# Graph network on one core: the second phase of the edge pass sums in PSUM over four node tiles per bank

## The reference, cut to what matters

```python
h = jnp.concatenate([x[row], edge_attr], axis=1)
h = jax.nn.relu(h @ W1a + b1a) @ W1b + b1b
sums = jax.ops.segment_sum(h, col, num_segments=n_nodes)
...
agg = sums / jnp.clip(counts, 1.0)[:, None]
z = jnp.concatenate([x, agg, u[batch]], axis=1)
return jax.nn.relu(z @ W2a + b2a) @ W2b + b2b
```

## Time and profile before

| what | us |
|---|---|
| median of 3 runs | 9276.49 (9272.69 to 9281.15) |
| profiled execution, its own time | 9279.41 |
| its span in the trace | 9277.6 |
| second block and tail, 8981.7 to the end | 295.9 |
| of it, the matmuls of the second block | 8995.5 to 9242.7 |
| TensorE busy in the whole span | 6981.1 (75%) |
| VectorE busy in the whole span | 5643.3 (61%) |
| ScalarE busy in the whole span | 2493.9 (27%) |
| mean granted clock of TensorE | 0.872 |

### The profile page before, as it was taken

How to read it: one execution, slowest core, us unless ns; L and a number is a source line. 1 busy time by engine, 2 the same in 40 slices (tenths; PEclk the granted TensorE clock), 3 DMA queues, 4 the chain that set the end, 5 groups by cost and what they waited for, 6 DMA issues and landing times. The chain is left out here.

```text
span 9277.6 us, 133405 instructions
## 1 busy us (share of the span) xinstructions
PE 6981.1 (75%) x35552; PEld 4550.7 (49%) x35552; DVE 5643.3 (61%) x16834; ACT 2493.9 (27%) x5841; POOL 2675.9 (29%) x2953
## 2 busy tenths in 40 slices
PE   4777777775566669960388779999998777777779
PEld 3555555543122224430277734444445666666668
DVE  6777777775589991039899920000012777777778
ACT  0222222222457750020288700000000333330000
POOL 0777777776461000000000000000001444444430
PEclk9776767776679999985699989999999999999999
DMA  3333333334975547849666658788887766762256
GB/s 99 100 104 105 104 105 104 105 103 140 392 257 165 166 123 276 300 171 426 245 215 215 193 192 282 250 295 272 269 282 229 181 181 179 180 159 63 64 98 197
DMA packets 969801, 1759.60 MB, mean 190 GB/s; under 512 B 102719, under 2 KB 665300, under 8 KB 905490
## 3 DMA queue, kind: packets, MB, share of 16 engines
q1 hardware_dynamic: 683996, 1335.60, 44.5%
q0 software_dynamic: 110720, 276.01, 9.2%
q10 hardware_dynamic: 174394, 139.51, 5.6%
HBM read 1411.91 MB, written 338.80 MB: 189 GB/s over the span
## 5 line engine op out<-in xcount | busy, mean ns | idle before, releaser
L768 POOL DMA_INDIRECT bucketed<-arena,wide x1563 | 1516.6, 970 | 729.9 <-issue 717.1
L1869 PE MATMUL psum<-wide,arena 128*128 x6496 | 1210.1, 329 | 401.2 <-DVE arena L1928 389.4
L1869 PEld LDWEIGHTS psum<-wide,arena 128*128 128x128 f32 x6496 | 988.5, 195 | 621.2 <-issue 494.9
L1738 POOL DMA_DIRECT2D table<-wide x13 | 9.7, 744 | 4325.3 <-DVE wide L1650 4325.3
L1928 DVE TENSOR_SCALAR arena<-wide,tile_first 128x128 f32 x3248 | 869.1, 301 | 471.2 <-PE psum L1869 298.2
L1790 POOL DMA_INDIRECT arena<-table,src_i x832 | 801.1, 963 | 1010.9 <-PE psum L1886 875.1
L1599 PE MATMUL psum<-arena,h 128*128 128x512 f32 (+1 forms) x2548 | 1049.5, 571 | 16.8 <-DMA arena<-adjacency 15.0
L922 PE MATMUL psum<-arena 128*128 128x512 bf16 x2304 | 698.1, 437 | 433.7 <-DVE arena L870 257.7
L665 PE MATMUL psum<-arena 128*113 128x177 bf16 x1568 | 532.4, 340 | 430.8 <-ACT wide L687 388.8
L870 DVE TENSOR_SCALAR arena<-sums 128x512 bf16<-128x512 int16 x2304 | 803.6, 349 | 0.0
L659 PE MATMUL psum<-w_edge,arena 128*128 128x256 f32 x1568 | 786.0, 597 | 0.0
(11 more groups left out here) (398 smaller groups left out, 10879.1 us busy)
## 6 DMA issues: line engine op xcount, KB each, us to landing
arena<-adjacency SPq DMA_DIRECT2D x294, 1024.0 KB
arena<-adjacency SPq DMA_DIRECT2D x98, 1568.0 KB, 7.8
adjacency<-wide SPq DMA_DIRECT2D x588, 256.0 KB
arena<-adjacency SPq DMA_DIRECT2D x196, 640.0 KB, 5.2
arena<-adjacency SPq DMA_DIRECT2D x147, 768.0 KB
arena<-bucketed POOLq DMA_DIRECT2D x208, 528.0 KB, 6.1
arena<-adjacency SPq DMA_DIRECT2D x49, 1792.0 KB, 6.8
arena<-adjacency SPq DMA_DIRECT2D x49, 1344.0 KB, 6.1
```

What stands on the lines that cost most here:

```text
L768: e.indirect_dma_start(bucketed, bass.IndirectOffsetOnAxis(ap=places[k][0:size, c:c + 1], axis=0), rows[k][0:size, c, :], None).then_inc(s ...
L1869: e.matmul(flat[:, ds((chunk & 3) * 512 + 2048, P)], lhsT=hot[:, i % 8, :], rhs=table_in[:, ds(tile * P, P)], start=False, stop=True, skip ...
```

## The change

TensorE now sums in PSUM over all pairs of a tile, and a bank of 512 columns holds the four tiles of a group. ScalarE fills a bank with the group's part of `h` ahead (`begin`), and copies it back to `h` when the last pair of the group is done. It waits for TensorE's count of pairs against a register; those 13 ends of groups (`group_end`) are computed by four new steps in `positions`. TensorE reads each pair's tile number into a register: two bits of it and the bits above give the column and the bank of the sum and the group that must be open. The first block of the edge pass is unchanged. VectorE has only the one-hots left, four pairs (eight chunks, 128 x 1024) in one instruction, in four buffers.

```diff
         last_i = sb("last_i", [1, TILES], i32)[:, :]
+        group_end = sb("group_end", [1, 16], i32)
...
+            ("vector", lambda e, _: e.tensor_copy(pair_end, last), 1),
             ("vector", lambda e, _: e.tensor_scalar(last, last, -1.0, 0.0, op0=ALU.add, op1=ALU.max), 1),
+            ("tensor", lambda e, _: e.matmul(psum[0:1, 1, 128:128 + TILES], lhsT=pair_end, rhs=ident[0:TILES, 0:TILES], start=True, stop=True), 1),
+            ("vector", lambda e, _: e.memset(group_end[:, GROUPS - 1:GROUPS], FAR_PAIRS + NEAR_PAIRS), 1),
+            ("vector", lambda e, _: e.tensor_scalar(group_end[:, 0:GROUPS - 1], psum[0:1, 1, 128 + GROUP - 1:128 + TILES - 1:GROUP], float(NEAR_PAIRS),
+                                                    float(FAR_PAIRS), op0=ALU.min, op1=ALU.add), 1),
...
                     for n in range(NEAR_PAIRS):
                         g = n // 2
+                        if n % DEEP == 0:
+                            _, tile = nc.values_load_multi_w_load_instructions(
+                                tile_i[0:1, n:n + DEEP], engines=(ENG.PE,), min_val=0, max_val=TILES - 1,
...
                         if n % 2 == 0:
                             e.wait_ge(near_got[g % DEEP].sem, near_got[g % DEEP].at + 16 * (g // DEEP) + 16)
-                        e.wait_ge(near_hot_done.sem, near_hot_done.at + n + 1)
-                        if n >= DEEP:
-                            e.wait_ge(near_add.sem, near_add.at + n - DEEP + 1)
+                        if n % QUAD == 0:
+                            e.wait_ge(near_hot_done.sem, near_hot_done.at + n // QUAD + 1)
+                        e.wait_ge(near_open.sem, (tile[n % DEEP] >> 2) + (near_open.at + 1))
                         for c in range(PAIR):
                             at = (n % 2 * PAIR + c) * P
-                            last = e.matmul(psum[:, n % DEEP, 0:P], lhsT=near_in[:, g % DEEP, at:at + P], rhs=near_hot[:, n % DEEP, c, :],
-                                            start=c == 0, stop=c == PAIR - 1)
+                            last = e.matmul(flat[:, ds((tile[n % DEEP] & 15) * P, P)], lhsT=near_in[:, g % DEEP, at:at + P],
+                                            rhs=near_hot[:, n // QUAD % 4, n % QUAD * PAIR + c, :], start=False, stop=True, skip_group_check=True)
                         last.then_inc(near_pe.sem, 1)

                 @block.vector
                 def _(e):
-                    def one_hots(n):
-                        if n >= DEEP:
-                            e.wait_ge(near_pe.sem, near_pe.at + n - DEEP + 1)
-                        e.tensor_tensor(near_hot[:, n % DEEP, :, :], iota[:, 0:P].unsqueeze(1).broadcast_to([P, PAIR, P]),
-                                        dst_f[:, cols(n)].unsqueeze(2).broadcast_to([P, PAIR, P]), ALU.is_equal).then_inc(near_hot_done.sem, 1)
-
-                    def add(n, tile):
-                        e.wait_ge(near_pe.sem, near_pe.at + n + 1)
-                        if n:
-                            e.wait_ge(near_add.sem, near_add.at + n)
-                        to = h[:, ds(tile, 1), :].rearrange("p a n -> p (a n)")
-                        e.tensor_tensor(to, to, psum[:, n % DEEP, 0:D], ALU.add).then_inc(near_add.sem, 1)
...
+                    for n in range(0, NEAR_PAIRS, QUAD):
+                        if n >= 4 * QUAD:
+                            e.wait_ge(near_pe.sem, near_pe.at + n - 3 * QUAD)
+                        e.tensor_tensor(near_hot[:, n // QUAD % 4, :, :], iota[:, 0:P].unsqueeze(1).broadcast_to([P, QUAD * PAIR, P]),
+                                        dst_f[:, cols(n, QUAD)].unsqueeze(2).broadcast_to([P, QUAD * PAIR, P]), ALU.is_equal).then_inc(near_hot_done.sem, 1)
+
+                @block.scalar
+                def _(e):
+                    def begin(g):
+                        a, n = dst_groups[g]
+                        e.copy(psum[:, g % 4, 0:n], part(h, a, n)).then_inc(near_open.sem, 1)
+
+                    for g in range(4):
+                        begin(g)
+                    _, end = nc.values_load_multi_w_load_instructions(
+                        group_end[0:1, 0:GROUPS], engines=(ENG.Activation,), min_val=FAR_PAIRS, max_val=PAIRS,
...
+                    for g, (a, n) in enumerate(dst_groups):
+                        e.wait_ge(near_open.sem, near_open.at + g + 1)
+                        e.wait_ge(near_pe.sem, end[g])
+                        e.copy(part(h, a, n), psum[:, g % 4, 0:n]).then_inc(near_closed.sem, 1)
+                        if g + 4 < GROUPS:
+                            e.wait_ge(near_closed.sem, near_closed.at + g + 1)
+                            begin(g + 4)
```

More of the change, by code:

```diff
@@ L384, in build @@
         last = held[0:TILES, 206:207]
+        pair_end = held[0:TILES, 207:208]
         last_i = sb("last_i", [1, TILES], i32)[:, :]
+        group_end = sb("group_end", [1, 16], i32)
         tot_i = held[0:TILES, 210:211].bitcast(i32)
@@ L1773, in edge_pass, with cols @@
             reason = "made by this program from its own counts of edges"
-            def cols(pair):
-                return slice(pair * PAIR, pair * PAIR + PAIR)
+            def cols(pair, n=1):
+                return slice(pair * PAIR, (pair + n) * PAIR)
             def bank(c):
@@ L1953, in edge_pass @@
             near_in = part(arena, 0, DEEP * 2 * PAIR * P).rearrange("p (k w) -> p k w", k=DEEP)
-            near_hot = part(arena, DEEP * 2 * PAIR * P, DEEP * PAIR * P).rearrange("p (k c w) -> p k c w", k=DEEP, c=PAIR)
+            near_hot = part(arena, DEEP * 2 * PAIR * P, 4 * QUAD * PAIR * P).rearrange("p (k c w) -> p k c w", k=4, c=QUAD * PAIR)
             near_got = [Baton(s_side[k], 16 * (FAR_PAIRS // DEEP)) for k in range(DEEP)]
-            near_hot_done, near_pe, near_add = Baton(s_hot, FAR_PAIRS), Baton(s_pe, FAR_PAIRS), Baton(s_add, FAR_PAIRS + 1)
+            near_hot_done, near_pe, near_open, near_closed = Baton(s_hot, FAR_PAIRS), Baton(s_pe, FAR_PAIRS), Baton(s_add, FAR_PAIRS + 1), Baton(s_msg, FAR_PAIRS)
             with nc.Block() as block:
@@ L1974, in _ @@
                         g = n // 2
+                        if n % DEEP == 0:
+                            _, tile = nc.values_load_multi_w_load_instructions(
+                                tile_i[0:1, n:n + DEEP], engines=(ENG.PE,), min_val=0, max_val=TILES - 1,
+                                skip_runtime_bounds_check_because="number of the 49 buckets that start at or before a pair, less one")
                         if n % 2 == 0:
                             e.wait_ge(near_got[g % DEEP].sem, near_got[g % DEEP].at + 16 * (g // DEEP) + 16)
-                        e.wait_ge(near_hot_done.sem, near_hot_done.at + n + 1)
-                        if n >= DEEP:
-                            e.wait_ge(near_add.sem, near_add.at + n - DEEP + 1)
+                        if n % QUAD == 0:
+                            e.wait_ge(near_hot_done.sem, near_hot_done.at + n // QUAD + 1)
+                        e.wait_ge(near_open.sem, (tile[n % DEEP] >> 2) + (near_open.at + 1))
                         for c in range(PAIR):
                             at = (n % 2 * PAIR + c) * P
-                            last = e.matmul(psum[:, n % DEEP, 0:P], lhsT=near_in[:, g % DEEP, at:at + P], rhs=near_hot[:, n % DEEP, c, :],
-                                            start=c == 0, stop=c == PAIR - 1)
+                            last = e.matmul(flat[:, ds((tile[n % DEEP] & 15) * P, P)], lhsT=near_in[:, g % DEEP, at:at + P],
+                                            rhs=near_hot[:, n // QUAD % 4, n % QUAD * PAIR + c, :], start=False, stop=True, skip_group_check=True)
                         last.then_inc(near_pe.sem, 1)
@@ new lines, in _ @@
+                @block.scalar
[7 more added lines that the diff above has]
+                        group_end[0:1, 0:GROUPS], engines=(ENG.Activation,), min_val=FAR_PAIRS, max_val=PAIRS,
+                        skip_runtime_bounds_check_because="number of pairs up to the end of four buckets of nodes")
+                    for g, (a, n) in enumerate(dst_groups):
[5 more added lines that the diff above has]
+                            begin(g + 4)
```

## The result

The changed kernel takes 9230.35 us (median of 6 runs, 9225.36 to 9241.5) against 9277.1 for the kernel before (6 runs): a ratio of 0.9946, 95% interval 0.9933 to 0.9959. That is 46.8 us, 0.5% faster, and inside the range of 9220 to 9300 that I gave; my middle of 9256 was 26 us too slow. The profiled execution took 9234.66, its span is 9232.8.

A forecast was written before the change was run, and what follows sets the result against it. VectorE was taken to pace the second block, with TensorE's sequencer pacing it after the change. Block -21.6, start +0.8, end -0.9 and `positions` +0.9 sum to -20.8 us: 9256 us, range 9220 to 9300.

The forecast's parts named there:

- What bounded the kernel before: Second block's matmuls: VectorE sets the pace, 4.70 us for each group of eight pairs.
- The mechanism that I forecast: Second block: TensorE's sequencer, with operations and register loads, sets the pace, 4.29 us for eight pairs; -21.6 us, chance 0.58.
- rival A: Second block: sequencer is cheaper, TensorE's array leads at 3.55 us for eight pairs; 185 to 200 us, 9216 to 9231; chance 0.17.
- the count of operations: TensorE's sequencer, each pair: four operations, namely shift, add, mask, and one fused multiply and add; 0.43 us a pair.
- The price of an operation: TensorE's sequencer: about 0.11 us for each register operation, not their own durations of 32 to 60 ns.
- the sign that I had set for A: Second block in the profile after: groups of eight pairs 3.6 us apart would show rival A.
- Rival B: Second block: second matmul works out its address again, two more operations, 0.22 us a pair; 317 us, 9347; chance 0.18.
- Rival C: Second block: handover of banks or the loads hold TensorE for 10 us; 9262 to 9272; chance 0.07.
- The start: Start of the second block: the first one-hot, held behind GpSimd's instruction, is longer; +0.8 us.
- `positions`: Four new steps in the relay, three on VectorE and one matmul, with nothing overlapping; +0.9 us.
- The end: From second block to tail: one short ScalarE copy follows instead of sums queued on VectorE; -0.9 us (0 to -1.2).
- The 11 us that I named as a bound: ScalarE's fills and copies in the second block: cost if uncovered, two copies for each of nine reused banks.

The follow-up runs named there:

- e2: Against e1, the second matmul of each pair computes its bank address anew, three register operations more a pair: block 394.5 us against 262.9, total 11,183.1 us.
- e3: Against e1, TensorE waits for an opened bank once for four pairs: block 225.4 us, total 10,996.5 us.
- e1: The changed kernel with registers that waits compare with loaded as low half words: block 262.9 us, total 11,033.8 us, 1.085 times the kernel before on that chip.
- e6: Against e5, TensorE waits for an opened bank once for eight pairs: block 188.7 us, time 9293.3 us.
- e8: e5 with one wait for eight pairs, the bias addition moved from GpSimd to VectorE, and only seven groups filled and copied back: 9273.05 us.
- e5: The changed kernel, whole words, with a maximum with 0 on each loaded value that a wait compares with: 9298.5 us, 1.0022 of the kernel before.
- e9: The changed kernel with the far half's two lists as adjacent 16-bit words, maxima only on the adjacency's and near half's waits: ratio 1.0489, second block 196.6 us.
- e4: Against e1, ScalarE fills and copies back only the seven groups this input's near half touches: 11,031.0 us against 11,033.8.

## Why the prediction came out as it did

**What bounded the kernel before** was right: VectorE. With its sums gone the block lost 51 us, and its one-hots of 1.23 us (1.226 measured) leave it 64 us of waiting for TensorE.

**That the time lies in the range is in part luck.** The mechanism that I forecast would have given 9256. The range holds 9230 because it was drawn wide enough for most of rival A, and a second miss, at the end, hides 6.0 of the 29.7 us by which the block was better.

**The step that failed is the count of operations**, "the shift, the add of the constant" as two: they are one. I had seen only masks stand alone in the earlier trace rows and carried that over to the shift. The price of an operation was right: I took 0.11 us, e2 and e3 give 0.105 and 0.12. The runs give a sum for the sequencer of a pair. e1 is 262.9 / 416 = 0.632 us; take away a load of 1.92 / 8 = 0.240 and 3.25 instructions (three operations, a quarter of an EVENT_SEMAPHORE) at 0.105, 0.341, and 0.051 is left. With a load of 0.59 the changed kernel comes to 0.051 + 0.341 + 0.074 = 0.466 us, 194 us in all, and some 2 us for the half clock at the start: 196, measured 195.9. A fourth operation would have made it, an estimate by the same sum, 0.571 and about 239 us, a gain of 8 us instead of 51. So one fused instruction decided between "hardly" and "0.5%".

The records show the same without a fit. In the changed kernel the sequencer's records start, in the median, 0.125 us (shift and add to mask), 0.093 (mask to address) and 0.125 (address to the next pair) apart, 0.106 after an EVENT_SEMAPHORE and 0.650 after a load: 3.61 us for eight pairs. All distances together are 195.1 us, of which 7.9 are over the medians, so the sequencer hardly ever waits for the array. In e6 it does: there 142 of 312 distances from an address to the next mask are longer, by 0.19 us in the mean.

The sum was a little short besides. With three operations my own prices gave 3.4 us for eight pairs (rival A), less than the array's 3.55; measured are 3.73 (195.9 less 2 us, over 52). What was missing is the 0.051 us a pair that is no operation. (And 52 x 4.29 + 2 is 225.1, not the 225.6 of the prediction; the slip of 0.5 us changes nothing.)

**Rival A is what happened**, at a chance of 0.17: 185 to 200 us, 9216 to 9231. Groups of eight pairs come 3.73 us apart, near the sign that I had set for A (3.6) and far from the forecast's (4.3). Its words "the array is the bound" aren't quite right. The array needs 0.444 us, the sequencer 0.466; e6 shows the 8 us between them, and e1 that every further load shows.

**Rival B** was wrong by its condition (one address for both matmuls), and right by its price: 0.21 us for two operations, as e2 bears out. **Rival C** didn't occur: neither banks nor loads held TensorE in the block.

**The start**, forecast +0.8, is +1.1. **`positions`**, forecast +0.9: from the step of line 420 to `last_i` it was 0.74 us and is 1.61, +0.87.

**The end**, forecast -0.9, is +5.1: the second step that failed. I costed ScalarE's copies as "beside TensorE's work" for all 13 groups at 32 pairs each, and didn't ask where this half's pairs lie. They fill six groups, some 66 pairs each, and begin a seventh (9.2 us of matmuls, from ScalarE's copy at 9183.65 to that at 9192.85); the others have no pair to hide behind. The 11 us that I named as a bound were for TensorE waiting for refills within the block; none of that came. What came is 4.8 us of copies behind the last pair, where 1.7 us had been before, and 1.7 us for the low clock of the tail's first 16 matmuls (3.75 instead of 2.02).

Together: forecast -20.8, profiled -44.75. Block 29.7 us better than forecast, end 6.0 worse; the barrier ahead of the block came only 0.2 us later, though `positions` took its 0.9.

**What stays open.** The three edits of e8 in the kernel as changed, without the maxima, weren't run. From e8's 25.4 us I would estimate 9205 us. (The edit to seven groups holds for this input's counts only.) Which of e5's two maxima costs the far half its 64 us wasn't separated. No kernel that was run beats the changed one.

## What to carry to other kernels

Where a matmul's address or wait comes from a register, count the sequencer's instructions for it at about 0.09 to 0.125 us each (0.105 to 0.12 in the mean of e2 and e3), not at the 32 to 67 ns of their records, and look at which of them fuse: arithmetic in a row did, masks did not. Compare the sum with the array. A wait moved to every eighth item gave 8 us here (e6), with values that never fall from item to item. And when work is said to be hidden behind other work, ask of the last items, and of items that have none, what they hide behind.

## What of the hardware was unexpected

- Eight 16-bit words take 1.83 to 1.92 us to load into registers, eight 32-bit words 0.59 (e1, e9); on ScalarE four 16-bit words take 0.89 us and four 32-bit words 0.31.
- A maximum with 0, fused with a shift and an add, costs the block at most 0.9 us over 416 pairs (e5); a maximum standing alone in the far half's loops (1624 on VectorE, 832 on ScalarE) goes with 64 us over 3248 look-ups.
- After 5.2 us without a matmul the tail's first 16 matmuls ran at a granted clock of 0.50 and took 3.75 us; after 1.0 us of pause (e4), or 1.75 (the kernel before), they had the full clock and 2.02 us.
- On TensorE an EVENT_SEMAPHORE's record is 51 ns, and the next one starts 0.106 us after it; the records of a mask are 32 ns, and the next starts after 0.093.
- In e2 the block's granted clock was 0.88, with TensorE's records covering 299.5 of 394.5 us; in e1 it stayed at 0.99 with 201.0 of 262.9.
